# Graph network with a mixture of experts: column tiles for gathered edges, 19 dense buckets, earlier edge counts

## The chip, the cores and the metric

One core of one Trainium2 chip runs the whole model in one program. The metric is device time in microseconds of one execution. The engines are called PE (matrix products), DVE (vector), ACT (activations), POOL (GpSimd; it also writes the descriptors of indirect DMAs) and SP (it issues the plain DMAs).

## The reference, cut to what matters

There are 6250 nodes with 256 features and 100000 edges sorted by their destination. The edge list is the same in all edge stages.

```python
x = x + (segment_sum(w[:, None] * (ln(x) @ w_nbr)[src], dst) + ln(x) @ w_own + bias)   # first edge stage
x = x + moe(ln(x))                    # router, best 2 of 8 experts, 256 -> 1024 -> 256
h = ln(x)
for i in range(3):                    # three convolution passes
    t = h @ W[i]
    h = segment_sum(t[row] * norm[:, None], col, n) + b[i]   # edges and one loop per node
    h = relu(layernorm(h) * gamma[i] + beta[i])
x = x + h
x = x + slice_attention(ln(x))
```

The norm is the product of the inverse roots of both ends' degrees. All is float32.

## The kernel before

**Tiling.** Nodes lie in NT = 49 tiles ("buckets") of 128; edges, in order of destination, in ET = 782 tiles of 128. A gathered edge tile costs one indirect DMA by POOL (128 rows of 1 KB of `table`, by `step_src`), a one-hot of the destinations made by DVE (`lane` equal to `step_dst`), and one matmul on PE that multiplies the transposed one-hot with the rows. G = 4 edge tiles in a row add up in one bank; they can touch two buckets, so DVE adds the bank twice into `ACC` with two masks (`add_group`), at an offset that `bucket_offsets` loads into registers.

**Stages in order.** `prologue` turns the lists, computes the first table and counts whether the lists fit the fixed plan (`bad`, `apart`; here they do). `first_steps` runs the first edge stage over all 782 edge tiles (`steps_and_route`; ring of 32 row slots) with the router beside it; SP clears the count matrix `A` in pieces there (`clear`). `mixture` is `place` (slot numbers), `invert` (lists by slot) and `experts` (56 blocks of 256 slots; PE on two layers, POOL fetches tokens and puts results). `convolutions` begins with `combine` and then runs `layers_hybrid`; `slices` is the last part.

**Dense buckets.** The first F = 17 buckets of a pass are not gathered. `A` in DRAM holds for each of them the edge counts between every source tile and the bucket. POOL builds it by indirect DMAs that add 128 ones each (`edges`, in `experts`, 4 chains, 264 of them; the places come from `dense_places` on DVE in the first block). In a pass SP loads pieces of 7 matrices (`piece`, 8 buffers) and PE multiplies them with the scaled features kept in `X`: 17 x 49 = 833 matmuls a pass.

**The order in a pass.** `layers_hybrid` writes the order of each engine out by the steps s from TD = 264 to 781, one gathered tile each; there are GT = 518. `quota(s)` says how many dense matmuls are done by step s: 40 ahead, the rest evenly to DENSE_END = 738. `batches` gives each pair of buckets a step `at` after its last edge or its bank; from there DVE runs the node work in fixed distances (sums, statistics, root on ACT, scale, shift), PE the `turns` at `at + 14` and `products` at `at + 18`, SP the `store` of the next table at `at + 21`, and the `refill` of `X`. PE's queue is in program order. The row ring has RG = 24 slots, freed by four matmuls at a time; POOL starts the next pass when all of the next table has been stored. The last pair of buckets is worked on after the last step.

## Time and profile before

| | us |
|---|---|
| runs, median of 3 | 4598.39 (4594.6 to 4601.92) |
| profiled execution, its own time | 4596.34 |
| its span | 4594.6 |
| PE busy | 3891.9 (85%) |
| POOL busy | 2871.1 (62%) |
| DVE busy | 2100.5 (46%) |
| ACT busy | 866.6 (19%) |
| mean granted clock of PE | 0.91 |

The span runs from the first to the last instruction of the profiled execution. A busy share is an average over stages whose limits differ, so the views by stage and by time are read beside it. An indirect DMA is shown on POOL with the time in which POOL writes its descriptors; the transfer itself is not in it. A float32 matmul appears as two recorded matmuls, and their ends are modelled, so starts say more than durations.

### The profile page before, as it was taken

To read this page: it belongs to the slowest core of one execution; us is meant where nothing else is said; L and a number is where in the kernel's file an instruction comes from. 1 tells how busy PE (TensorE), PEld (TensorE's weight loads), DVE (VectorE), ACT (ScalarE), POOL (GpSimd) and SP (SyncE) were. 2 spreads that over 40 slices of the span, in tenths; PEclk is the share of its full clock that TensorE was granted. 3 is DMA by queue.
4 is the path that set the end of the run, shared out by engine and by line. 5 is a ranking of instruction groups with operands and counts; after the bars stand their busy time and mean duration, and the time that the engine had idled before them with its cause. 6 is when DMAs were issued, how large, how long until landed. Compare 5 with 4: busy or idle time off the path is not lost. (4 is left out here: it accounts for less than half of the span.)

```text
span 4594.6 us, 52816 instructions
## 1 busy us (share of the span) xinstructions
PE 3891.9 (85%) x16777; PEld 3209.9 (70%) x16777; DVE 2100.5 (46%) x6813; ACT 866.6 (19%) x2121; POOL 2871.1 (62%) x2846
## 2 busy tenths in 40 slices
PE   5656666666699999995899998999998999995988
PEld 4544444444488888884788887888886877774657
DVE  5444444454611111116345455454554555555974
ACT  1233333333122222223001011001011000000322
POOL 0377777777168778880677776777776777774000
PEclk8877677777799999997999999999998999997998
DMA  3355555555266666668766666666666666662001
GB/s 106 105 170 168 168 167 164 168 168 167 65 181 188 190 188 188 192 171 272 227 203 200 204 199 208 207 202 202 201 204 204 206 202 204 199 188 69 0 12 57
DMA packets 422939, 779.23 MB, mean 170 GB/s; under 512 B 106971, under 2 KB 264194, under 8 KB 422722
## 3 DMA queue, kind: packets, MB, share of 16 engines
q1 hardware_dynamic: 255078, 433.81, 29.0%
q0 software_dynamic: 160992, 336.12, 26.3%
q10 hardware_dynamic: 6652, 6.67, 0.5%
q8 instruction: 104, 1.70, 0.2%
q14 instruction: 113, 0.93, 0.1%
HBM read 655.55 MB, written 114.39 MB: 168 GB/s over the span
## 5 line engine op out<-in xcount | busy, mean ns | idle before, releaser
L2142 POOL DMA_INDIRECT rows_h<-table,step_src x1554 | 1487.7, 957 | 638.1 <-issue 562.0
L2182 PE MATMUL bank_g<-X,piece_h 128*128 128x256 f32 x4998 | 1314.3, 380 | 14.3 <-DMA piece_h<-edges_A 14.3
L2182 PEld LDWEIGHTS bank_g<-X,piece_h 128*128 128x128 f32 x4998 | 952.0, 190 | 144.8 <-issue 14.7
L2197 PE MATMUL bank_g<-rows_h,hot_h 128*128 128x256 f32 x3108 | 939.7, 390 | 77.6 <-DMA rows_h<-table,step_src 76.9
L887 POOL DMA_INDIRECT rows_r<-table,step_src x782 | 743.1, 950 | 359.3 <-issue 339.2
L912 PE MATMUL bank_r<-rows_r,hots_r 128*128 128x257 f32 x1564 | 578.7, 531 | 382.3 <-ACT rows_r L897 382.0
L2238 DVE TENSOR_SCALAR hot_h<-lane,step_dst 128x128 f32<-128x128 f32 x1554 | 458.6, 302 | 838.4 <-PE bank_g L2197 812.0
L912 PEld LDWEIGHTS bank_r<-rows_r,hots_r 128*128 128x128 f32 x1564 | 394.2, 266 | 546.2 <-ACT rows_r L897 456.0
L2197 PEld LDWEIGHTS bank_g<-rows_h,hot_h 128*128 128x128 f32 x3108 | 591.9, 194 | 193.9 <-DMA rows_h<-table,step_src 116.2
L923 DVE TENSOR_SCALAR hots_r<-lane,step_dst 128x128 f32<-128x128 f32 x782 | 233.9, 306 | 503.2 <-PE bank_r L912 488.9
L1704 POOL DMA_INDIRECT edges_A<-one_d,place_d x264 | 413.4, 1566 | 80.5 <-issue 80.5
L897 ACT ACTIVATE rows_r<-rows_r,step_w 128x256 f32<-128x256 f32 x782 | 339.7, 498 | 639.3 <-DMA rows_r<-table,step_src 639.2
L1663 PE MATMUL pH_e<-xe_e,w_e 128*128 128x256 f32 x1792 | 397.7, 380 | 2.5 <-DMA b_e<-in_L_ffn_b 2.5
L1678 PE MATMUL pY_e<-w_e,h_e 128*128 128x256 f32 x1792 | 396.0, 379 | 0.0
L956 DVE SCALAR_TENSOR_TENSOR ACC<-bank_g,mask,ACC 128x256 f32 x780 | 339.5, 477 | 102.7 <-issue 80.8
L1663 PEld LDWEIGHTS pH_e<-xe_e,w_e 128*128 128x128 f32 x1792 | 341.6, 191 | 49.6 <-issue 2.9
L1678 PEld LDWEIGHTS pY_e<-w_e,h_e 128*128 128x128 f32 x1792 | 336.1, 190 | 43.4
L1638 ACT ACTIVATE h_e<-pH_e,prm_e 128x256 f32<-128x256 f32 x448 | 187.8, 470 | 630.6 <-PE pH_e L1663 630.6
L1606 DVE TENSOR_SCALAR xe_e<-pT_e,prm_e 128x256 f32<-128x256 f32 x114 | 56.7, 539 | 372.6 <-PE pT_e L1670 362.8
L2219 ACT ACTIVATE sd_g<-mv_g,eps 128x2 f32<-128x2 f32 (+1 forms) x75 | 22.1, 295 | 1016.3 <-DVE mv_g L2266 1016.3
L1623 DVE TENSOR_TENSOR y_e<-pY_e,b_e 128x256 f32<-128x256 f32 x112 | 42.3, 419 | 322.4 <-PE pY_e L1678 322.4
L956 DVE SCALAR_TENSOR_TENSOR ACC<-bank_r,mask,ACC 128x257 f32 x392 | 170.7, 477 | 18.0 <-issue 15.3
(318 smaller groups left out, 3039.7 us busy)
## 6 DMA issues: line engine op xcount, KB each, us to landing
piece_h<-edges_A SPq DMA_DIRECT2D x357, 448.0 KB, 3.6
w_e<-in_L_ffn_W SPq DMA_DIRECT2D x112, 1024.0 KB, 8.1
edges_A<-zero_r SPq DMA_DIRECT2D x119, 448.0 KB, 4.9
rows_h<-table,step_src POOLq DMA_INDIRECT x1554, 3.3
got_c<-y SPq DMA_DIRECT2D x14, 896.0 KB, 9.6
rows_r<-table,step_src POOLq DMA_INDIRECT x782, 2.8
table<-ACC SPq DMA_DIRECT2D x48, 256.0 KB
X<-table SPq DMA_DIRECT2D x12, 896.0 KB, 12.1
```

The lines of the kernel that those rows point to most:

```text
L887: nc.gpsimd.indirect_dma_start(out=r["rows"][:, x, 0:D], out_offset=None, in_=r["table"][:, :], in_offset=bass.IndirectOffsetOnAxis(ap=c[" ...
L897: act.activation(r["rows"][:, x, 0:D], r["rows"][:, x, 0:D], ACT.Copy, scale=c["step_w"][:, k:k + 1]).then_inc(r["s_scaled"], 1)
L912: pe.matmul(psum[k // G % OH][:, 0:AW], r["hots"][:, k % HOTS, :], r["rows"][:, k % R, 0:AW], start=(k % G == 0), stop=(k % G == G - 1 or ...
L923: v.tensor_scalar(r["hots"][:, k % HOTS, :], c["lane"][:, :], c["step_dst"][:, k:k + 1], None, ALU.is_equal).then_inc(r["s_hot"], 1)
L956: v.scalar_tensor_tensor(out=a, in0=bank[:, 0:width], scalar=c["mask"][:, k, g:g + 1], in1=a, op0=ALU.mult, op1=ALU.add).then_inc(c["ring" ...
L1663: mm = pe.matmul(pH[j][:, n * BR:(n + 1) * BR], w1[:, q, k, o:o + P], xe[:, q, k, :], start=(k == 0), stop=(k == KD - 1))
L1678: mm = pe.matmul(pY[m][:, 0:D], h[:, j, m * P:(m + 1) * P], w2[:, q, j, :], start=(j == 0), stop=(j == HJ - 1))
L1704: nc.gpsimd.indirect_dma_start(out=dram["A"][:, :], out_offset=bass.IndirectOffsetOnAxis(ap=d["place"][:, col:col + 1], axis=0), in_=d["on ...
L2142: nc.gpsimd.indirect_dma_start(out=d["rows"][:, x, :], out_offset=None, in_=tables[l - 1][:, :], in_offset=bass.IndirectOffsetOnAxis(ap=c[ ...
L2182: mm = pe.matmul(pD[o % 2][:, 0:D], d["piece"][:, n % AB, x % PC, :], c["X"][:, ORDER[x // PC] * PC + x % PC, :], start=(x == 0), stop=(x ...
L2197: pe.matmul(pS[i // G % OH][:, 0:D], d["hot"][:, i % HOTS, :], d["rows"][:, x, :], start=(i % G == 0), stop=(i % G == G - 1 or i == GT - 1 ...
L2238: v.tensor_scalar(d["hot"][:, i % HOTS, :], c["lane"][:, :], c["step_dst"][:, TD + i:TD + i + 1], None, ALU.is_equal).then_inc(r["s_hot"], 1)
```

## The change

1. **Column tiles.** In the three passes a one-hot has 32 columns (destination modulo 32, `step_low`). Groups have GB = 8 edge tiles; two in a row (GP = 2) go to one of four column positions of the array (`tile_position`), so four sums of 32 lanes stand in one bank (`lanes`). DVE copies the bank to `mid` and makes a one-hot `spread` from `target`, the bucket lane of each of the 128 partial rows (`kept`); PE multiplies them (`spread`), which puts the rows in their lanes, and DVE adds the product twice with masks (`added`). There are 61 groups a pass. The prologue makes `step_low` and `target` and checks the list for this form.
2. **Buckets.** F = 19, TD = 296, GT = 486 gathered tiles, 931 dense matmuls a pass, ending at step 754. Node work moves: turns at `at + 8`, products at `at + 10`, store at `at + 14`. The first five refills are issued one by one as the last bucket's matmuls pass, and no longer together after it.
3. **Edge counts.** 296 scatters. Ten are issued in `place`, 23 in `invert`, 263 in `experts`. `dense_places` runs in the first edge stage; SP loads its lists there; 133 pieces are cleared over the first 23 of 25 batches.
4. **Combining** is pipelined by a group: sums of group g + 1 come before the normalisation of group g; a refill of `X` by ACT copies takes the place of a DMA.

```diff
-F = 17
+F = 19
-GG = -(-GT // G)
+GB, GP = 8, 2
+GG = -(-GT // GB)
+LOW = P // 4
-DENSE_END = 738
+DENSE_END = 754
+EARLY = (10, 33)
...
+                elif t == 7:
+                    then(v.tensor_scalar(base_i[:, 0, :], base[:, 0, :], -1.0, part[:, 0:1], ALU.mult, ALU.add))
+                    then(v.tensor_scalar(base_i[:, 1, :], base_i[:, 0, :], LOW - 1, None, ALU.bitwise_and))
+                    then(v.tensor_copy(base[:, 1, :], base_i[:, 1, :]))
+                    then(v.tensor_tensor(base_i[:, 0, :], base[:, 0, :], base[:, 1, :], ALU.add))
+                    then(v.tensor_scalar(base_i[:, 1, :], base_i[:, 0, :], P - 1, None, ALU.bitwise_and))
+                    v.tensor_copy(c["target"][:, :], base_i[:, 1, :])
...
         @block.gpsimd
         def _(g):
+            numbers(nc, d)
             run_pool(nc, c, r, g)
...
+                if i == LAG and u == 12:
+                    dense_places(v, c, d)
...
+            g.wait_ge(c["s_clear"], 16 * PIECES)
+            for n in range(EARLY[0]):
+                edges(nc, g, dram, d, n)
...
+            for n in range(*EARLY):
+                edges(nc, g, dram, d, n)
...
+            def kept(g):
+
+                act.wait_ge(c["s_x2"], 16 * (g + 1))
+                act.wait_ge(q["h"], g * TG + TG)
+                for t in range(g * TG, (g + 1) * TG):
+                    i = act.activation(c["X"][:, t, :], c["ACC"][:, t, 0:D], ACT.Copy)
+                i.then_inc(c["s_hd"], 16)
...
+            added(0)
+            for g in range(NG):
+                if g + 1 < NG:
+                    added(g + 1)
+                normalised(g)
...
-                        if l < LAYERS and s == at + 21:
+                        if l < LAYERS and s == at + 14:
                             store(l, k)
...
-                    if i % Q == 0 and i >= RG:
-                        g.wait_ge(r["s_mm"], n - RG + Q)
+                    if i % GB == 0 and i >= RG:
+                        g.wait_ge(r["s_mm"], n - RG + GB)
...
+            def lanes(l, h):
+
+                n, tiles = ET + (l - 1) * GT, tiles_of(h)
+                m = (l - 1) * GG + h
+                for x in sorted({i % RG // Q for i in tiles}):
+                    last = max(i for i in tiles if i % RG // Q == x)
+                    pe.wait_ge(r["s_row"][x], 16 * (BEFORE[x] + (l - 1) * EACH[x] + landed(last, GT, RG, x)))
+                pe.wait_ge(r["s_hot"], n + tiles[-1] + 1)
+                if m >= 2:
+                    pe.wait_ge(d["s_mid"], m - 1)
+                for i in (*tiles[0::GP], *tiles[1::GP]):
+                    k = i % GB // GP * LOW
+                    pe.matmul(pA[m % 2][k:k + LOW, 0:D], d["hot"][:, i % (2 * GB), :], d["rows"][:, i % RG, :],
+                              start=(i % GP == 0), stop=(i % GP == GP - 1), tile_position=(0, k)).then_inc(r["s_mm"], 1)
+
+            def spread(l, h):
+
+                m, k = (l - 1) * GG + h, rows_of(h)
+                pe.wait_ge(d["s_mid"], m + 1)
+                if m >= 2:
+                    pe.wait_ge(r["s_add"], 2 * (EG + m - 1))
+                pe.matmul(pR[m % 2][:, 0:D], d["spread"][0:k, m % 2, :], d["mid"][0:k, m % 2, :],
+                          start=True, stop=True).then_inc(d["s_spread"], 1)
...
+                    s = TD + i
+                    if i % GB == 0:
+                        lanes(l, i // GB)
+                        if i >= GB:
+                            spread(l, i // GB - 1)
                     dense(l, AHEAD_MM if i == 0 else quota(s - 1), quota(s))
                     if l < LAYERS:
                         for k, (_, _, at) in enumerate(GROUPS):
-                            if s == at + 14:
+                            if s == at + 8:
                                 turns(l, k)
-                            if s == at + 18:
+                            if s == at + 10:
                                 products(l, k)
+                spread(l, GG - 1)
...
+            def kept(l, h):
+
+                m, k = (l - 1) * GG + h, rows_of(h)
+                v.wait_ge(r["s_mm"], ET + (l - 1) * GT + tiles_of(h)[-1] + 1)
+                v.tensor_scalar(d["spread"][:, m % 2, :], c["lane"][:, :], c["target"][:, h:h + 1], None, ALU.is_equal)
+                v.tensor_copy(d["mid"][0:k, m % 2, :], pA[m % 2][0:k, 0:D]).then_inc(d["s_mid"], 1)
...
+                    s, h = TD + i, i // GB
+                    if i % GB == 0 and h >= 1:
+                        kept(l, h - 1)
+                        if h >= 2:
+                            added(l, h - 2)
+                    if i + GB < GT:
+                        hot(i + GB)
```

## Rows read from the trace of the kernel before

**Rows 1.** The page: busy tenths in 40 slices, two engines.
```profile
PE   5656666666699999995899998999998999995988
...
POOL 0377777777168778880677776777776777774000
```

**Rows 2.** Windows by stage: us, busy us (instructions) by engine, PEclk, DMA share, GB/s.
```profile
1242.30:2081.00 838.70, 805.62 (x3812) 702.37 (x3812) 114.78 (x297) 189.04 (x449) 637.10 (x491) 0.99 0.67 185
2081.00:2199.50 118.50, 70.43 (x296) 51.60 (x296) 77.56 (x252) 49.23 (x112) 0.00 (x0) 0.80 0.88 288
2199.50:2872.50 673.00, 650.17 (x3010) 568.23 (x3011) 332.64 (x1073) 62.96 (x172) 495.88 (x518) 0.98 0.68 207
```

**Rows 3.** The page, groups: busy us, mean ns, idle before and its releaser.
```profile
L2142 POOL DMA_INDIRECT rows_h<-table,step_src x1554 | 1487.7, 957 | 638.1 <-issue 562.0
...
L1704 POOL DMA_INDIRECT edges_A<-one_d,place_d x264 | 413.4, 1566 | 80.5 <-issue 80.5
```

**Rows 4.** Timeline, POOL: start us, us, line, operation, idle before; gathers at pass ends.
```profile
2199.56 0.99 POOL L2142 DMA_INDIRECT rows_h<-table,step_src  x1 [126.95 <-issue]
...
2852.03 0.95 POOL L2142 DMA_INDIRECT rows_h<-table,step_src  x1 [0.30 <-issue]
2872.57 0.94 POOL L2142 DMA_INDIRECT rows_h<-table,step_src  x1 [19.59 <-DMA table<-ACC]
```

**Rows 5.** Timeline, PE: back to back in pass 1, and after a wait.
```profile
2610.71 0.59 PE L2197 MATMUL bank_g<-rows_h,hot_h 128*128 128x256 f32 x2
2611.14 0.59 PE L2182 MATMUL bank_g<-X,piece_h 128*128 128x256 f32 x2
...
4201.61 1.13 PE L2197 MATMUL bank_g<-rows_h,hot_h 128*128 128x256 f32 x4 [0.16 <-DMA rows_h<-table,step_src]
```

**Rows 6.** Groups by line of PE alone, 2223 to 2816 us (dense part of pass 1).
```profile
L2182 PE MATMUL bank_g<-X,piece_h 128*128 128x256 f32 x1589 | 420.5, 379 | 0.0
L2197 PE MATMUL bank_g<-rows_h,hot_h 128*128 128x256 f32 x949 | 282.4, 379 | 0.0
L2165 PE MATMUL bank_g<-w_g,xt_h 128*128 128x256 f32 x168 | 39.7, 379 | 0.0
L2155 PE MATMUL bank_g<-ident,xin_h 128*128 128x128 f32 x84 | 12.6, 273 | 0.0
```

**Rows 7.** Timeline, PE: first gathered matmuls of passes 1 and 2.
```profile
2223.41 0.59 PE L2197 MATMUL bank_g<-rows_h,hot_h 128*128 128x256 f32 x2
...
2886.78 0.59 PE L2197 MATMUL bank_g<-rows_h,hot_h 128*128 128x256 f32 x2
```

**Rows 8.** Timeline, all engines: the end of pass 1.
```profile
2855.07 1.06 PE L2155 MATMUL bank_g<-ident,xin_h 128*128 128x128 f32 x4
...
2856.16 0.66 ACT L2227 ACTIVATE xt_h<-bank_g 128x256 f32<-128x256 f32 x2 [10.34 <-PE bank_g L2155]
...
2857.41 1.89 PE L2165 MATMUL bank_g<-w_g,xt_h 128*128 128x256 f32 x8
...
2858.64 0.88 DVE L956 SCALAR_TENSOR_TENSOR ACC<-bank_g,mask,ACC 128x256 f32 x2 [0.24 <-DVE ACC L956]
```

**Rows 9.** Timeline, DVE: list work in the prologue.
```profile
54.31 0.54 DVE L389 CAST lane_i_a<-dcol 128x782 int32<-128x782 f32 x1
...
65.25 0.97 DVE L409 TENSOR_TENSOR falls<-now_i,next_i 128x782 f32<-128x782 int32 x1 [2.22 <-DMA deg_i<-in_dst]
```

**Rows 10.** Timeline, POOL and DVE: constants and ends of placing and inversion, an iota.
```profile
1176.83 0.29 POOL L1383 TENSOR_SCALAR_AFFINE_SELECT before<-ones 128x128 f32<-128x128 f32 x1
...
1194.75 0.19 DVE L1464 TENSOR_SCALAR moe_expert<-ebf 128x57 int32<-128x57 f32 x1
...
1241.78 0.22 DVE L1529 TENSOR_SCALAR moe_put<-dest_i 128x112 int32<-128x112 f32 x1
...
1242.27 0.36 POOL L1708 IOTA aside_d<- 128x264 f32 x1 [46.56 <-POOLq L1472]
```

**Rows 11.** Timeline, DVE: after ACT's root in the last group of the combining.
```profile
2178.79 0.20 DVE L1821 RECIPROCAL rs_g<-sd_g 128x7 f32<-128x7 f32 x1 [2.41 <-ACT sd_g L1858]
```

More of the change, by code:

```diff
@@ L68 @@
 GT = ET - TD
-GG = -(-GT // G)
+GB, GP = 8, 2
+GG = -(-GT // GB)
+LOW = P // 4
+EP = -(-ET // GP)
 RG = 24
@@ L97, in batches @@
 def batches():
-    out = [(t, 2, 16 * (t + 2) + SLACK) for t in range(F, NT - 2, 2)]
+    out = [(t, 2, 16 * (t + 2) + 2 * GB) for t in range(F, NT - 2, 2)]
     taken = [s for _, _, s in out]
@@ L103, in batches @@
         s = bucket_done(t + n - 1) + 3
-        while min(abs(s - x) for x in taken) < 12:
+        while min(abs(s - x) for x in taken) < 10:
             s += 1
@@ L154, in build @@
             prologue(nc, ins, dram, c, sb, pb, sem)
+            d = dict(place=sb("place_d", [P, TD], I32, g), one=sb("one_d", [P, TD], F32, g), s_ed=sem("d_ed"), s_ix=sem("d_ix"),
+                     s_acc=[sem(f"d_acc{k}") for k in range(CHAINS)])
             apart = nc.values_load(c["apart"][0:1, 0:1], min_val=0, max_val=1,
@@ L327, in _ @@
             pe.wait_ge(s_kept, 1)
-            pe.matmul(pH[:, 0:EG], firsts[:, :], dcol[:, 0:EG * G:G], start=True, stop=True).then_inc(s_head, 1)
+            pe.matmul(pH[:, 0:EP], firsts[:, :], dcol[:, 0:EP * GP:GP], start=True, stop=True).then_inc(s_head, 1)
             turn(0)
@@ L1020, in token_rows, with numbers, route_sync @@
     sp.dma_start(rows[:, bass.ds(t, n), :], c["X"][:, bass.ds(t, n), :]).then_inc(q["rows"], 16)
-def route_sync(sp, ins, dram, moe, b, q):
+def numbers(nc, d):
+    nc.gpsimd.iota(d["aside"][:, :], [[1, TD]], base=0, channel_multiplier=TD,
+                   allow_small_or_imprecise_dtypes=True).then_inc(d["s_ed"], 16)
+def route_sync(sp, ins, dram, moe, b, d, q):
+    for name in ("src", "dst"):
+        sp.dma_start(d[name][:, :], ins[name][0:ED].rearrange("(p n) -> p n", p=P)).then_inc(d["s_ed"], 16)
     sp.dma_start(b["wr"][:, :, :], ins["L0_ffn_Wr"].rearrange("(k p) e -> p k e", p=P)).then_inc(q["w"], 16)
@@ L1263, in _ @@
             sp.wait_ge(c["s_clear"], 16 * PIECES)
+        @block.gpsimd
+        def _(g):
+            numbers(nc, d)
         @block.vector
@@ L1341, in _, with place @@
                     mm.then_inc(q["L"], 1)
-def place(nc, c, moe, sb, pb, sem):
+def place(nc, dram, c, moe, d, sb, pb, sem):
     with ExitStack() as ctx:
@@ L1544, in _, with edges, experts @@
             body(NG - 1)
-def experts(nc, ins, dram, c, moe, sb, pb, sem):
+def edges(nc, g, dram, d, n):
+    k, x = n // CHAINS, n % CHAINS
+    col = x * (TD // CHAINS) + k
+    if k == 0:
+        g.wait_ge(d["s_ix"], PLACED)
+    else:
+        g.wait_ge(d["s_acc"][x], 16 * k)
+    nc.gpsimd.indirect_dma_start(
+        out=dram["A"][:, :], out_offset=bass.IndirectOffsetOnAxis(ap=d["place"][:, col:col + 1], axis=0),
+        in_=d["one"][:, col:col + 1], in_offset=None, compute_op=ALU.add).then_inc(d["s_acc"][x], 16)
+def experts(nc, ins, dram, c, moe, d, sb, pb, sem):
     with ExitStack() as ctx:
@@ L1697, in results @@
                         in_=y[:, b % 2, m, :], in_offset=None).then_inc(s_st[b % 2], 16)
-            def edges(n):
-                k, x = n // CHAINS, n % CHAINS
-                col = x * (TD // CHAINS) + k
-                wait(g, s_acc[x], 16 * k)
-                nc.gpsimd.indirect_dma_start(
-                    out=dram["A"][:, :], out_offset=bass.IndirectOffsetOnAxis(ap=d["place"][:, col:col + 1], axis=0),
-                    in_=d["one"][:, col:col + 1], in_offset=None, compute_op=ALU.add).then_inc(s_acc[x], 16)
-            nc.gpsimd.iota(d["aside"][:, :], [[1, TD]], base=0, channel_multiplier=TD,
-                           allow_small_or_imprecise_dtypes=True).then_inc(s_ed, 16)
             for b in range(4):
@@ L1806, in convolutions @@
                          xt=sb("xt_h", [P, 2, D], F32, own))
-                d.update(rows=sb("rows_h", [P, RG, D], F32, own), hot=sb("hot_h", [P, HOTS, P], F32, own),
+                d.update(rows=sb("rows_h", [P, RG, D], F32, own), hot=sb("hot_h", [P, 2 * GB, LOW], F32, own), mid=sb("mid_h", [P, 2, D], F32, own),
+                         spread=sb("spread_h", [P, 2, P], F32, own),
                          piece=sb("piece_h", [P, AB, PC, P], F32, own), bank=bank)
@@ L2070, in dinv, with tiles_of, rows_of @@
         return c["dinv"][:, t:t + 1]
+    def tiles_of(h):
+        return range(h * GB, min(h * GB + GB, GT))
+    def rows_of(h):
+        return -(-len(tiles_of(h)) // GP) * LOW
     def used(l, s):
@@ L2258, in stats @@
                 v.wait_ge(q["z"], (l - 1) * NT + FIRST[k] + n)
+                if l == LAYERS and k > 0:
+                    v.wait_ge(q["zz"], 3 * FIRST[k])
                 for u in range(n):
@@ L2350, in _ @@
                         nodes(l, k, s - at)
+                for h in range((GT + 1) // GB, GG):
+                    kept(l, h)
+                for h in range((GT + 1) // GB - 1, GG):
+                    added(l, h)
                 v.wait_ge(r["s_add"], 2 * (EG + l * GG))
```

208 lines of the change are left out of this document (115 added, 93 removed).

## The prediction

> **What bounds the kernel now.** I read the slices of the page first. PE is at 8 to 9 tenths from the expert stage on, and POOL stands at 7 wherever it issues indirect DMAs [rows 1]. Both look busy and neither looks full, so the slices don't settle it. The windows by stage give the sizes: the experts 839 us, the combining 118.5 us, then three convolution passes alike, of which the first has 673 us at a granted clock of 0.98 [rows 2]. The change lies mostly in the three passes, so I looked there for what ends last.
>
> POOL issues one gather per edge tile. One takes 957 ns [rows 3], and the next starts after 0.30 us: 1.25 us from start to start, without a stall. Pass 1 runs from its first gather at 2199.56 to its last at 2852.03, that is 652.5 us for 517 intervals, 1.262 us each [rows 4]; the passes 2 and 3 have the same 518 gathers at the same mean, and I count three times 652.5, 1957.5 us. The 562 us of "issue" ahead of the gathers [rows 3] look like idle time, but most of it is this 0.30 us, paid 1,500 times. POOL therefore sets the passes. Between two passes it stands still, 20.54 us from start to start, waiting for the table to be stored [rows 4].
>
> PE is hardly less loaded. One 128x128 by 128x256 float32 matmul is two recorded matmuls, and the next one starts 0.43 us later (2610.71 to 2611.14; its pair takes 0.59 us, which is 2 x 0.216 and a tail of 0.16) [rows 5]. From 2223 to 2816, the dense part of pass 1, no PE group has any idle time before it [rows 6]. That stretch holds 793 dense and 474 gathered matmuls and node work for 42 tiles. Node work is 8 halves a pair (1.73 us) and 4 half transposes (about 0.44 us), so 1.08 us a tile and 45 us in all; (593 - 45) / 1267 = 0.4325 us a matmul, the same number again. So PE has no reserve either: POOL leads, PE is just full. That is the reason why a cheaper gathered matmul counts here and why more dense work alone would not pay.
>
> **The passes.** Two buckets more go from gathered to dense. TD goes from 264 to 296, so gathers fall from 518 to 486 per pass. If POOL still leads, a pass is 485 x 1.262 = 612.1 us, and three are 1836.3 instead of 1957.5 us: 121.2 us less.
>
> Now PE. In eight steps POOL needs 10.1 us. PE has to do: dense, 891 matmuls over 458 steps, 15.56 x 0.4325 = 6.73 us (now 13.38, 5.79 us); nodes, about 45 tiles x 1.08 over 57 groups, 0.85 us; one new spread matmul, 0.43 us. These make 8.02 us. To it comes the group of eight gathered tiles, each now a matmul with 32 stationary columns, placed in four column positions. The trace has no matmul in a column tile, so its cost is bounded. From above: nothing overlaps, eight times 0.4325 is 3.46 us, since the moving side still streams 256 columns. From below: four abreast, 0.87 us. I take two abreast, 8 x 0.216 and one more half, 1.95 us, because each float32 product is two halves on one column tile, the second half follows the first, and only the neighbour's first half can run beside it. It is an assumption; the nearest row is the back-to-back pair of halves [rows 5].
>
> Going from full to column use and back may empty the array. After a wait four halves took 1.13 us [rows 5] instead of 4 x 0.216 = 0.86 (tail included), so a restart is 0.27 us. A group has none, one or two of them; I take one. Then eight tiles cost 2.2 us and PE needs 10.24 us per eight steps.
>
> The rows show a tail and a restart price, but nothing that changes the shape of the array. The Trainium skill, "TensorEngine Tiling (Array Packing)", section "Tiling Modes", says that changing the tiling mode drains the engine; that speaks against the change and asks for both restarts, a rival below. The Trainium skill, "TensorE: Matmul & The Clock Gate", section "Part 3: Packing small matmuls", gives 2.38x for three column tiles; worked out from that page, an estimate, eight tiles would be 1.45 us, and every pass would stay with POOL. No row here shows either.
>
> A pass lasts, if PE leads, from the first gather: PE's lag at its first gathered matmul (2223.41 - 2199.56 = 24 us in pass 1, 2886.78 - 2872.57 = 14 us later [rows 4, 7]), plus 57 groups, plus about 8 us for the last six gathers, which wait for slots of the ring of 24. Pass 1: 24 + 57 x 10.24 + 8 = 616 us, against 612 of POOL. Pass 2: 606 us, so POOL's 612.1. Pass 3 has no transposes and products, 9.39 us per group: POOL. Sum 1840 us, a gain of 117.5 us. What covers the 98 dense matmuls more in a pass (42 us) is only the cheap group; if that cover goes, they are on the path at once.
>
> DVE: one-hots of 32 columns in place of 128 are no dearer than 0.30 us, and per eight steps it now adds one group pair instead of two; two new operations (about 0.7 us) replace them. It has time. New waits: DVE waits for a whole group of matmuls before it copies (the hot tiles of the next group are issued before that, so PE is not starved), PE's spread waits for that copy one group later, SP's refills wait for bank use in five steps. Queued behind SP's waits are the pieces, with eight buffers, 28 steps of dense work. I cost these waits at nothing while PE's group takes 10 us. DMA in the passes is at 0.68 [rows 2]; the bytes rise a few per cent in less time, to about 0.75, hidden likewise.
>
> **The ends of the passes.** Now the turns of the last but one pair run while rows are awaited, and the last add starts at 2858.64 [rows 8]. After the change PE's order is: last group, spread of the group before, turns and products of the pair due at 768, and only then the last spread. From the end of the last group that is 0.43 + 1.1 (four half transposes) + 0.66 and 0.2 (ACT copy) + 1.89 (products) [rows 8] and 0.6 for the spread, 4.9 us; before, the add came about 1 us after the last matmul. The chain from there to the next gather is as before. 4.2 us more, twice: +8.4. After pass 3 there are no products: +1.
>
> **The rest.** Prologue: DVE runs without a break there and gets about a dozen operations more: two of 486 columns (below the 0.54 us of one of 782 [rows 9]), wider head copies, a chain of six at about 0.2 us. About 4.5 us, of which a DMA wait takes 2.2 us [rows 9]: +2.5 (0 to +5). First pass: one iota ahead of the gathers, +0.4 [rows 10]; the place arithmetic moved there from the experts is 5 us of DVE under a POOL that never waits, and 14 more clears go over SP at a DMA load of about half: nothing. Slots: ten scatters at 1.57 + 0.30 us [rows 3] make 18.7 us behind POOL's constants, which end at 1177.12; so 1195.8, and DVE is done at 1194.94 [rows 10]: +1.3. Inversion: 23 scatters, 43 us from 1195.7, end at 1239, while DVE ends at 1242.0 [rows 10]: nothing, at most +4 if full DVE work slows POOL. Experts: 263 scatters instead of 264, 4.87 a block at 1.87 us and four other DMAs of about 1.28 us, 14.2 us of POOL in 15.0 us a block (839 / 56 [rows 2]), as now; iota gone ahead of the first fetch: -0.7.
>
> Combining: DVE idles 2.4 us per group for ACT's root [rows 11], seven times. The pipelining takes that out, but ACT gets 49 copies (2.8 us a group) in place of a DMA, and has about 7 x 1.2 us of its own a group. So ACT takes over the pace at 12 to 12.5 us, where about 13.5 us a group stand now (118.5 us [rows 2] less some 24 us ahead of and behind the seven). An extra 9 us of filling at the start eats most of it. -3, from -12 to +5.
>
> Sum: -117.5 + 8.4 + 1 + 2.5 + 0.4 + 1.3 - 0.7 - 3 = -107.6. The profiled execution took 4596.34 us (span 4594.6), 2 us below the median of 4598.39. So 4488.7; I say 4489.
>
> **The rivals.** *Serial column tiles*: the change doesn't do what it says, matmuls in different column positions run one after another. Eight tiles cost 3.46 us and one restart, 3.73. PE per group 11.75 us: pass 1 702, pass 2 692, pass 3 (10.9 us) 644, in sum 2038, +80.5; with the other terms 4686 us (4640 without restarts, 4731 with two). It decides from 3.2 us per eight tiles, 0.40 us a tile: above it the kernel is slower. For it speaks that 0.4325 is what the streaming of the moving operand costs in this trace at any weight; against it, that weight loads already run beside matmuls. Chance 0.19.
> *Half the overlap*: eight tiles at 2.9 us, PE leads in passes 1 and 2 (654 and 645 us), pass 3 612: gain 46.5, time 4560. Chance 0.14.
> *Both restarts*, the mechanism of the drain, full to column and back, each 0.27 us: PE 10.5 us per group, passes 631, 620 and 612, time 4512. Chance 0.15.
> *POOL leads throughout* (up to four abreast, no restart seen) is within the forecast: 4485. Forecast with it 0.52.
>
> **How the numbers follow.** Forecast 4489, from 4467 (all passes with POOL, prologue free, combining -12) to 4510. Adding the second and third rival brings the held chance to 0.8; the range is 4467 to 4562. About 0.2% (9 us) is what a measurement tells from no change. Slower by more than that: the serial case less its edge, 0.18. Within: 0.04, the stretch near 0.40 us a tile. Faster: 0.78.
>
> **What would show it.** POOL's gathers still 1.26 us apart to the end of each pass, 612 us from first to last: right. Gathers that wait for PE, in passes 1 and 2 but not in 3: PE leads, and starts of PE's column matmuls a half apart (0.216) or less, 0.11, or a full 0.43 tell which rival. The gap between passes at 24.7 us. No scatter ending after DVE in the inversion. I would be wrong if gathers slow down by themselves at the higher DMA load, or if PE waits for DVE's copies.

## The result and the profile after the change

The changed kernel takes 4487.34 us (median of four runs, 4485.14 to 4489.91), the kernel before 4596.5 us beside it (4593.27 to 4601.92): a ratio of 0.9762 with a 95% interval of 0.9745 to 0.9778. The profiled execution has a span of 4487.6 us against 4594.6 before, 107.0 us less. The forecast was 4489.

The page, the busy tenths of two engines and the granted clock in 40 slices; [rows 1] has the same slices of before:

```profile
PE   5656555656589999996799998899997888885988
POOL 0377777777657778774277777577776777773000
PEclk9887778777799999998999999899998999997988
```

They look like those of before, and that is the first thing to read: the same engines work at the same shares, over a shorter time. Groups by line (busy us, mean ns | idle before, and what ended it); the gathers answer to [rows 3], the rest to [rows 6]:

```profile
L2233 POOL DMA_INDIRECT rows_h<-table,step_src x1458 | 1393.7, 956 | 613.9 <-issue 565.4 <-DMA table<-ACC 48.2 <-PE bank_g L2290 0.3
L2273 PE MATMUL bank_g<-X,piece_h 128*128 128x256 f32 x5586 | 1262.3, 382 | 11.7 <-DMA piece_h<-edges_A 11.7
L2290 PE MATMUL bank_g<-rows_h,hot_h 128*32 128x256 f32 x2916 | 213.5, 410 | 195.4 <-issue 187.9 <-DMA rows_h<-table,step_src 7.1
L2299 PE MATMUL bank_g<-mid_h,spread_h 128*128 128x256 f32 (+1 forms) x366 | 141.4, 472 | 0.0
```

GpSimd (POOL) issues 1458 gathers instead of 1554 at the same 956 ns. In all three passes it waits 0.3 us for TensorE (PE) and 48.2 us for the table between passes, and for nothing else: it leads ("issue" is its own 0.30 us between two gathers, and the time ahead of the first). TensorE has 195.4 us of idle time ahead of the gathered products (L2290). The profile puts most of it down to "issue"; it is the wait for rows: at the end of pass 1 the last gather starts at 2813.00, the page has 3.6 us from a gather's issue to its landing, and the last group starts at 2816.55. From 2223 to 2816 us of pass 1 these waits are 43.7 us, where before had none in the same stretch [rows 6].

Windows of pass 1 with the gap behind it, and of 300 us in its middle (us, busy us and instructions of PE, PEld, DVE, ACT, POOL, then granted clock, DMA share, GB/s); [rows 2] has before's:

```profile
2201.80:2838.73 636.93, 575.65 (x3266) 457.74 (x3267) 252.90 (x1035) 62.97 (x172) 464.37 (x487) 0.96 0.72 222
2351.80:2651.80 300.00, 280.54 (x1628) 225.07 (x1627) 123.54 (x504) 32.02 (x88) 227.48 (x239) 0.99 0.72 218
```

TensorE is busy 280.5 of 300 us: GpSimd leads, and TensorE has 6 to 7% in reserve. The pass and its gap are 636.9 us, where 673.0 us stood.

Two groups of eight gathered tiles in that stretch, timeline of PE (start, duration, line):

```profile
2558.22 1.07 PE L2290 MATMUL bank_g<-rows_h,hot_h 128*32 128x256 f32 x16
2559.22 0.70 PE L2299 MATMUL bank_g<-mid_h,spread_h 128*128 128x256 f32 x2
2559.76 6.64 PE L2273 MATMUL bank_g<-X,piece_h 128*128 128x256 f32 x30
2566.32 1.07 PE L2290 MATMUL bank_g<-rows_h,hot_h 128*32 128x256 f32 x16
2567.33 0.70 PE L2299 MATMUL bank_g<-mid_h,spread_h 128*128 128x256 f32 x2
2567.86 4.48 PE L2273 MATMUL bank_g<-X,piece_h 128*128 128x256 f32 x20
```

The 16 halves of eight products take 1.07 us with their tail. Their starts come in fours: 0, 0.007, 0.013 and 0.020 us, then 0.240 to 0.260, 0.456 to 0.476, 0.672 to 0.692. Four positions of the array work side by side. The last dense half starts at 2566.02 and is due to be done with its 0.216 us at 2566.23, so the eight tiles hold TensorE for 1.09 us until the spreading product starts; 0.10 us more pass before the dense products go on (2567.33 + 2 x 0.216 = 2567.76, against 2567.86). So 1.20 us in all, changes between whole array and columns among it.

Where the 107 us are, by stage, from the starts in the two traces:

| stage | before | after | measured | forecast |
|---|---|---|---|---|
| to the first gather | 178.9 | 176.5 | -2.4 | +2.9 |
| first gathers (782) | 980.1 | 980.4 | +0.3 | 0 |
| last of them to the first expert product (slots, inversion) | 96.5 | 102.2 | +5.7 | +0.6 |
| experts, first to last product | 813.5 | 816.5 | +3.0 | 0 |
| combining, up to the first gather of pass 1 | 130.7 | 126.2 | -4.5 | -3 |
| three passes, first to last gather | 1957.5 | 1834.1 | -123.4 | -117.5 |
| two gaps between passes | 40.4 | 50.1 | +9.7 | +8.4 |
| behind the last gather | 397.1 | 401.6 | +4.5 | +1 |

### The profile page after: what moved, and what is told of

It is laid out like the page before. It is cut to its first block and busy times, and to the rows that moved or that the text cites. A ratio compares the mean times of both kernels' runs of the same rounds, so it can differ in the third digit from the quotient of the medians.

```text
span 4487.6 us, 54073 instructions
## 1 busy us (share of the span) xinstructions
PE 3621.3 (81%) x17539; PEld 2865.8 (64%) x17539; DVE 1868.7 (42%) x6689; ACT 873.3 (19%) x2164; POOL 2828.6 (63%) x2783
## 5 line engine op out<-in xcount | busy, mean ns | idle before, releaser
L2233 POOL DMA_INDIRECT rows_h<-table,step_src x1458 | 1393.7, 956 | 613.9 <-issue 565.4
L2273 PE MATMUL bank_g<-X,piece_h 128*128 128x256 f32 x5586 | 1262.3, 382 | 11.7 <-DMA piece_h<-edges_A 11.7
L2273 PEld LDWEIGHTS bank_g<-X,piece_h 128*128 128x128 f32 x5586 | 1070.3, 192 | 161.0 <-issue 13.3
L939 PE MATMUL bank_r<-rows_r,hots_r 128*128 128x257 f32 x1564 | 553.3, 511 | 410.0 <-ACT rows_r L924 409.6
L1604 POOL DMA_INDIRECT edges_A<-one_d,place_d x296 | 464.1, 1568 | 90.3 <-issue 90.3
L2290 PE MATMUL bank_g<-rows_h,hot_h 128*32 128x256 f32 x2916 | 213.5, 410 | 195.4 <-issue 187.9
L2350 DVE TENSOR_SCALAR hot_h<-lane,step_low 128x32 f32<-128x32 f32 x1458 | 274.2, 254 | 17.2 <-issue 17.2
L2290 PEld LDWEIGHTS bank_g<-rows_h,hot_h 128*32 128x32 f32 x2916 | 89.7, 113 | 292.5 <-issue 263.1
L2357 DVE TENSOR_SCALAR spread_h<-lane,target 128x128 f32<-128x128 f32 x183 | 56.1, 307 | 466.3 <-PE bank_g L2290 466.2
L983 DVE SCALAR_TENSOR_TENSOR ACC<-bank_g,mask,ACC 128x256 f32 x366 | 159.9, 479 | 76.6 <-issue 58.1
```

Source lines behind the costliest of these rows:

```text
L939: pe.matmul(psum[k // G % OH][:, 0:AW], r["hots"][:, k % HOTS, :], r["rows"][:, k % R, 0:AW], start=(k % G == 0), stop=(k % G == G - 1 or ...
L1604: nc.gpsimd.indirect_dma_start(out=dram["A"][:, :], out_offset=bass.IndirectOffsetOnAxis(ap=d["place"][:, col:col + 1], axis=0), in_=d["on ...
L2233: nc.gpsimd.indirect_dma_start(out=d["rows"][:, x, :], out_offset=None, in_=tables[l - 1][:, :], in_offset=bass.IndirectOffsetOnAxis(ap=c[ ...
L2273: mm = pe.matmul(pD[o % 2][:, 0:D], d["piece"][:, n % AB, x % PC, :], c["X"][:, ORDER[x // PC] * PC + x % PC, :], start=(x == 0), stop=(x ...
L2290: pe.matmul(pA[m % 2][k:k + LOW, 0:D], d["hot"][:, i % (2 * GB), :], d["rows"][:, i % RG, :], start=(i % GP == 0), stop=(i % GP == GP - 1) ...
L2350: v.tensor_scalar(d["hot"][:, i % (2 * GB), :], c["lane"][:, 0:LOW], c["step_low"][:, i:i + 1], None, ALU.is_equal).then_inc(r["s_hot"], 1)
```

## The experiments

Twelve kernels ran. Four of them (e5 to e8) had a chip on which the kernel before took 4597.3 us, as usual. The other eight had two chips on which it took 5050 us (e1 to e4) and 5079 us (e9 to e12); I call them disturbed. Their first stage, which no variant touches, lasted 1112 to 1121 us instead of 980. Their microseconds are therefore not compared with 4487, only their ratios to before on the same chip, and what their traces show of single engines. The changed kernel itself did not run on these two chips, so no ratio measured there can be set against the change's 0.9762. What is known of the disturbance stands at the end. Of the numbers that follow, those marked as ratios carry their 95% interval.

### Are four column tiles really four abreast?

e1 puts all gathered tiles in one column position:

```diff
-                for i in (*tiles[0::GP], *tiles[1::GP]):
-                    k = i % GB // GP * LOW
+                for i in tiles:
+                    k = 0
```

with `rows_of` returning `LOW`, so that the spreading product takes 32 rows alone.

> The changed kernel, but all gathered tiles in the first of the four column positions (no two can run side by side), written to the first 32 lanes of the bank; the spreading product takes those 32 lanes alone, so the aggregates of three quarters of the gathered tiles are wrong. If the eight lane products are cheap because four positions work at once (16 halves in 1.07 us, starts of four 7 ns apart, the next four 0.215 us later), the 16 halves now stand one behind the other: 16 x 0.215 = 3.4 us, 2.4 us more for each of 61 groups, 145 us more of TensorE per pass; TensorE then leads all three passes: 4740 us, 4700 to 4780. If the products are cheap for their 32 columns of weights and not for their positions, it stays at 4488.

Measured: 5004 us (two runs), ratio 0.991 (0.9877 to 0.9943). PE's timeline, and the window of pass 1 with its gap:

```profile
2614.59 3.64 PE L2290 MATMUL bank_g<-rows_h,hot_h 128*32 128x256 f32 x16
2618.16 0.69 PE L2299 MATMUL bank_g<-mid_h,spread_h 32*128 32x256 f32 x2
2341.24:3107.36 766.12, 738.73 (x3266) 523.51 (x3267) 251.87 (x1035) 63.09 (x172) 468.75 (x487) 0.98 0.60 185
```

The same 16 halves take 3.64 us, one behind the other with 0.216 us between starts. The 32 columns of weights save nothing; the four positions do. From the dense half before them to the one behind the spreading product a group costs 2.66 us more than with four positions. TensorE's recorded busy time for a pass and its gap is 738.7 us, but such times come out longer on the disturbed chips (more on that under e4), so I work the serial rival out from spacings, an estimate: 931 dense products at 0.4325 us, 61 groups at 3.86 us, 61 spreading products at 0.43 us and 53 us of node work (49 tiles at 1.08) are 717 us in passes 1 and 2, and 664 us in pass 3 without node work. The changed kernel needs 636.9, 634.0 and 613.3 us with all its waits. So TensorE would lead everywhere, and the kernel would take about 4700 us or more: the serial rival of the prediction was real as a mechanism. e10 is the same kernel once more:

> The kernel of one column position again (aggregates of three quarters of the gathered tiles wrong), since the chip of its first run held every kernel up at gathers that landed late: there a group of 16 halves took 3.64 us against 1.07 to 1.09 in four positions. By that price, 2.55 us more for each of 61 groups, 156 us more of TensorE in a pass, and it leads all three: passes with their gaps of 637 us become some 730, the third 680: 4740 us (4700 to 4780). If GpSimd's gathers still led, 4488.

It had a disturbed chip too: 5041 us, ratio 0.9931 (0.9902 to 0.9961), with 740.9 us of TensorE in pass 1. The total of this rival on an undisturbed chip was not measured.

e2 keeps the positions and issues the eight products in the order of the tiles, so that neighbours have the same position: `for i in tiles:` alone.

> The changed kernel with the eight lane products of a group issued in the order of the tiles, 0 1 2 ... 7, so that each two neighbours have the same column position. If TensorE starts products in the order of issue and one waits for the last of its position, the eight take five steps of 0.43 us instead of two: 2.2 us instead of 1.07, 1.2 us per group, 70 to 75 us of TensorE per pass; passes 1 and 2, with about 575 us busy in 637, become some 20 to 30 us longer each, the third hardly: 4540 us (4515 to 4560). If the order does not matter (the engine takes whichever position is free): 4488.

Measured: 5026 us, ratio 0.996 (0.9941 to 0.9979). PE's timeline:

```profile
2613.75 1.09 PE L2290 MATMUL bank_g<-rows_h,hot_h 128*32 128x256 f32 x16
```

1.09 us, not 2.2. The starts are again four together (0, 0.014, 0.027, 0.040, then 0.240 to 0.280). The first four halves in order of issue all have the same position here, and e1 shows that halves of one position start 0.216 us apart. So my picture, that a product waits at the head of one queue for its own position, is wrong: products of other positions behind it start beside it. The order of the tiles is not what gives the overlap. The time of the whole kernel settles nothing: 0.996 lies above what either case was to give (4540 and 4488 us are ratios of 0.988 and 0.976), and TensorE stood still for 139 of the 766 us of pass 1 with its gap. Whether the order costs something elsewhere stays open.

### Which part of the change pays?

e3 has everything but the two buckets:

```diff
-F = 19
+F = 17
...
-DENSE_END = 754
+DENSE_END = 738
```

> The changed kernel with 17 dense buckets as before (dense products ending at step 738), so: column tiles, early scatters and the new combining alone. If GpSimd's gathers lead every pass at 1.251 us a tile, 32 more tiles cost 40 us a pass, 120 us in three, and the column tiles alone give nothing: 4607 us (4595 to 4612), no faster than the kernel before. If the relief of TensorE alone had shortened a pass, it would be at 4560 or less.

Measured: 5077 us, ratio 1.0059 (1.0042 to 1.0076), on the disturbed chip; once more as e11:

> 17 dense buckets with the column tiles and all the rest of the change, again, on a chip where gathers land in time: 518 tiles at 1.251 us a pass instead of 486, 40 us a pass: 4600 us (4590 to 4610), the time of the kernel before within 0.3%. If column tiles shortened a pass by themselves: 4560 or less.

5111 us, ratio 1.0062 (1.0046 to 1.0079), on the other disturbed chip. Twice 0.6% slower than before: on these chips the column tiles with the early scatters and the new combining give nothing by themselves. I had expected within 0.3%; where the other 0.3% go I can't say. For a chip where gathers land in time the trace of before says the same: they already went out 1.262 us apart there [rows 4], and a cheaper product can't shorten that.

e4 has the two buckets and everything else, but the gathered path of before, one product of 128 columns per tile, with the node work at its old distances (turns at `at + 14`, products at `at + 18`, store at `at + 21`):

```diff
...
-                pe.matmul(pA[m % 2][k:k + LOW, 0:D], d["hot"][:, i % (2 * GB), :], ...
+                pe.matmul(pS[i // G % OH][:, 0:D], d["hot"][:, i % HOTS, :], d["rows"][:, x, :],
...
```

> The changed kernel with the gathered path of before (one product of 128 columns a tile, no lanes and no spreading, groups of four) and 19 dense buckets. If TensorE has no room for two more buckets without column tiles: 11.0 us of it for eight steps against 10.0 of GpSimd in passes 1 and 2, 664 and 654 us instead of 611 and 610, the third pass at GpSimd's 612, the two gaps between passes 4 to 5 us shorter each: 4575 us (4560 to 4595). If GpSimd leads here too: 4480, and the column tiles were not needed.

> 19 dense buckets with the gathered path of before, again, on a chip where gathers land in time: if TensorE leads passes 1 and 2 without the column tiles (11.0 us for eight steps against 10.0), 664 and 654 us instead of 611 and 610, gaps 4 to 5 us shorter: 4575 us (4555 to 4595). If GpSimd leads: 4480.

Measured: 4932 and 4956 us, ratios 0.9765 (0.9749 to 0.9781) and 0.9764 (0.9747 to 0.978). So on the disturbed chips two buckets more pay without column tiles, and nothing shows that column tiles help there: e2, the changed kernel but for its order of issue, stood at 0.996 on the chip on which e4 stood at 0.9765. GpSimd's gathers of a pass are 1.45 to 1.56 us apart on average in all of e1 to e4 and e9 to e12, not by their number alone: in e4's passes GpSimd waits 223.6 us for TensorE to free row slots and 104.5 us for a releaser that the profile calls "remote". Window of e4's pass 1 with its gap:

```profile
2345.30:3090.11 744.81, 697.34 (x3140) 596.83 (x3141) 302.90 (x1027) 62.77 (x172) 468.40 (x486) 0.97 0.62 190
```

TensorE is recorded busy for 697.3 us of it, for 689.2 in the next pass and 641.5 in the third. That can't be carried over to a chip where gathers land in time: e2, whose products are those of the changed kernel, has 627.3, 620.1 and 597.6 us on the same chip, where the changed kernel has 575.7, 576.1 and 518.8. From the 0.4325 us of the trace of before, an estimate: 931 + 486 products are 612.9 us and the node work of 49 tiles 52.9 us. So TensorE has at least 665.8 us of work in passes 1 and 2 and 612.9 in pass 3, against the 636.9, 634.0 and 613.3 us that the changed kernel needs with all its waits. TensorE would lead passes 1 and 2, and e4 would be at least 61 us above the changed kernel: 4548 us or more. With the 23 us in which TensorE stands still in pass 1 and its gap before ([rows 2]: 673.0 less 650.17) in both, it is 4594, the time of the kernel before; my 4575 lies between. That the column tiles are needed for more than half of the gain is therefore worked out, not run.

### What do the early scatters cost and give?

e5: `EARLY = (0, 0)`, all 296 scatters beside the experts.

> The changed kernel with all 296 edge-count scatters in the experts' stage, none ahead of it. GpSimd is nearly full there (616 us busy and 140 of issue in 774, 18 us waiting for VectorE): 33 more at 1.57 + 0.31 us are 62 us, 18 of them hidden: experts 44 us longer, and the slots' and the inversion's 5 to 6 us come back: 4526 us (4510 to 4545). If TensorE's experts hide them: 4481, and the early scatters cost time without need.

Measured: 4533.0 us (4527.1 to 4534.5), ratio 0.9861 (0.9846 to 0.9876), 45.7 us more than the change; the experts take 56.1 us more, the two stages ahead of them 6.2 less and the combining 4.4 less. GpSimd's timeline in the changed kernel (the last scatter beside the slots, the first constant of the inversion, the last scatter beside the inversion, the experts' first fetch), then in e5:

```profile
1192.91 1.56 POOL L1604 DMA_INDIRECT edges_A<-one_d,place_d  x1 [0.30 <-issue]
1196.66 0.24 POOL L1537 IOTA token<- 128x98 f32 x1 [2.19 <-ACTq L1519]
...
1239.18 1.59 POOL L1604 DMA_INDIRECT edges_A<-one_d,place_d  x1 [0.30 <-issue]
1247.09 1.01 POOL L1739 DMA_INDIRECT tok_e<-tokens,moe_inv  x1 [6.33 <-POOLq L1519]
```

```profile
1173.42 0.17 POOL L1420 IOTA node<- 128x49 f32 x1 [16.46 <-SPq L1391]
1192.35 0.24 POOL L1537 IOTA token<- 128x98 f32 x1 [18.10 <-ACTq L1519]
1240.05 0.98 POOL L1739 DMA_INDIRECT tok_e<-tokens,moe_inv  x1 [47.22 <-POOLq L1519]
```

Slots: 18.9 us from the constants to the inversion without scatters, 22.0 with ten (1174.63 to 1196.66). Inversion: 47.7 us without, 50.4 with 23. That is the +5.7 us of the table. Beside the slots the last scatter ends at 1194.47, 0.4 us after VectorE's last operation, and the inversion starts 2.2 us later; without scatters it starts 0.3 us after VectorE's last. In the inversion the scatters are over 6.3 us before the experts start, so GpSimd isn't late; what is late is VectorE. Its two operations that make the lists (L1559 and L1560, 98 each) take 309 and 382 ns on average beside the scatters, 277 and 329 in e5. Most are as quick as there, but in 20 of the 23 scatters one L1560 that starts some 0.54 us into it takes 0.59 us instead of 0.33, and one L1559 at 0.78 us takes 0.40 instead of 0.28. Waits of PE in the experts' stage, 1300 to 2060 us, in the changed kernel and in e5 (total us, times, longest):

```profile
PE pT_e L1721 <- DMA tok_e<-tokens,moe_inv: 10.9, 15, 1.7
```

```profile
PE pT_e L1721 <- DMA tok_e<-tokens,moe_inv: 50.3, 35, 3.6
```

With all scatters there TensorE waits 50.3 us for its tokens, and the stage takes 872.6 us instead of 816.5: 1.70 us for each of 33 scatters, nearly the full 1.87 of one. I had expected 44 us for the stage, with 18 hidden; 56 came. It works on the other side too: with 231 scatters instead of 263 (e3, e11) the stage took 802.0 and 801.9 us on the disturbed chips, where every kernel with 263 took 815 to 819. So GpSimd is partly on the path of the experts in the changed kernel as well, and 32 scatters fewer would be worth up to 14.5 us there.

### The combining, and the last spreading product

e6 puts the combining stage of before into the changed kernel.

> The changed kernel with the combining stage of before (one moments buffer, each group added and normalised in turn, the residual copied by DMA). The traces have the stage at 133.2 us after and 137.6 before: 4492 us (4490 to 4494), 0.1% longer. If that difference came from the stages around it: 4487.

Measured: 4494.5 us (4493.1 to 4498.7), ratio 0.9783 (0.977 to 0.9797), 7.2 us more. In its trace the stage takes 130.7 us, as before, against 126.2: the 4.5 us of the table come from the combining's own code. The other 2.7 us have no place in the trace and are within what runs differ by.

e7 issues the last spreading product one step after its lanes:

```diff
+                    if i == (GT - 1) // GB * GB + 1:
+                        spread(l, GG - 1)
-                spread(l, GG - 1)
```

> The changed kernel with the last spreading product of a pass issued one step after its lanes, ahead of the node products of the pair due at step 768, instead of behind them. In the trace that product starts 6.1 us after the one before it, behind two node operations, one of 3.75 us: if it is on the path that ends a pass, each of the two gaps between passes is 4 to 5 us shorter, the step after the third pass 0 to 2: 4478 us (4475 to 4483). If the node products' pair is late instead and takes its place: 4487.

Measured: 4483.7 us (4480.7 to 4486.5), ratio 0.9759 (0.9746 to 0.9773), 3.7 us less by the medians, which the runs alone don't tell from nothing (the intervals of the two ratios overlap nearly whole). The trace does: the gaps are 22.4 and 21.5 us instead of 25.7 and 24.4, 6.2 us less together. The end of pass 1 in the changed kernel, then in e7:

```profile
2816.55 1.93 PE L2290 MATMUL bank_g<-rows_h,hot_h 128*32 128x256 f32 x12 [5.18 <-issue]
2818.41 1.22 PE L2299 MATMUL bank_g<-mid_h,spread_h 128*128 128x256 f32 x2
2819.42 1.06 PE L2246 MATMUL bank_g<-ident,xin_h 128*128 128x128 f32 x4
...
2820.95 3.75 PE L2256 MATMUL bank_g<-w_g,xt_h 128*128 128x256 f32 x8 [0.47 <-ACT xt_h L2339]
2824.53 0.61 PE L2299 MATMUL bank_g<-mid_h,spread_h 96*128 96x256 f32 x2
2825.28 0.88 DVE L983 SCALAR_TENSOR_TENSOR ACC<-bank_g,mask,ACC 128x256 f32 x2 [4.63 <-PE bank_g L2299]
...
2838.73 0.94 POOL L2233 DMA_INDIRECT rows_h<-table,step_src  x1 [24.79 <-DMA table<-ACC]
```

```profile
2813.00 1.93 PE L2290 MATMUL bank_g<-rows_h,hot_h 128*32 128x256 f32 x12 [4.79 <-issue]
2816.73 1.06 PE L2299 MATMUL bank_g<-mid_h,spread_h 96*128 96x256 f32 x2
2817.58 2.39 PE L2256 MATMUL bank_g<-w_g,xt_h 128*128 128x256 f32 x8
2817.93 0.88 DVE L983 SCALAR_TENSOR_TENSOR ACC<-bank_g,mask,ACC 128x256 f32 x2 [0.83 <-PE bank_g L2299]
2831.91 0.95 POOL L2233 DMA_INDIRECT rows_h<-table,step_src  x1 [21.50 <-DMA table<-ACC]
```

From the last lanes to the last add it was 8.7 us and is 4.9. The order of two instructions is worth 3 us a gap; of the 3.8 us in the first gap 0.5 are given back behind it.

### How far does it go?

e8 has 21 dense buckets, and the 32 further scatters in a new GpSimd block of the combining stage, where it was idle:

```diff
-F = 19
+F = 21
...
+COMBINED = 32
...
-            late = TD - EARLY[1]
+            late = TD - EARLY[1] - COMBINED
...
+        @block.gpsimd
+        def _(g):
+            for n in range(TD - COMBINED, TD):
+                edges(nc, g, dram, e, n)
...
```

The wait for the end of all scatters moves there too.

> The changed kernel with 21 dense buckets; the 32 further scatters stand in the combining stage, where GpSimd is idle. If GpSimd's gathers lead the passes at 1.251 us with TensorE close behind: 32 tiles fewer, 40 us a pass, 4368 us. If TensorE takes the lead in passes 1 and 2 (575 us busy, 37 more of dense products, 8 less of lanes, 605 against a pass and gap of 597 at GpSimd's pace): about 17 us gained in each of these and 40 in the third, 0 to 10 lost in combining: 4415 us (4405 to 4435). This one is the forecast.

Measured: 4396.9 us (4394.5 to 4400.6), ratio 0.9569 (0.9554 to 0.9584), 90.4 us below the changed kernel and below my range. Windows inside passes 1 and 2, and GpSimd's waits in the passes:

```profile
2370.00:2570.00 200.00, 200.00 (x1145) 162.50 (x1143) 81.30 (x328) 23.00 (x63) 144.95 (x152) 1.00 0.74 225
2985.00:3185.00 200.00, 200.00 (x1142) 162.73 (x1145) 77.29 (x316) 21.91 (x60) 151.68 (x159) 1.00 0.76 231
POOL rows_h L2239 <- issue: 407.1, 1336, 0.5
POOL rows_h L2239 <- DMA table<-ACC: 51.2, 2, 25.8
POOL rows_h L2239 <- PE bank_g L2296: 31.6, 23, 2.3
```

TensorE is busy 200 us of 200, and GpSimd now waits for it, 31.6 us in 23 places. The passes are 589.0, 579.2 and 575.2 us, where the gathers alone would take 453 x 1.251 = 567. So TensorE has the lead in passes 1 and 2 at 21 buckets, as expected, but it costs less of the gain: 22 and 30 us came off them, not 17 each. And the combining hides its 32 scatters whole (126.5 us against 126.2). This is the test of what leads: 32 gathers fewer per pass bring 22, 30 and 38 us, of 40.

e9 is e8 with the order of e7 and `AHEAD_MM = 54` instead of 40.

> 21 dense buckets with the 32 further scatters in the combining stage, the last spreading product of a pass ahead of the pair's node products, and 54 instead of 40 dense products ahead of a pass's first gathered tile. With 21 buckets TensorE was busy without a gap in the middle of passes 1 and 2 (200 us of 200), so what is moved into the gap before the pass comes off it: 14 x 0.38 = 5 us in each of the first two passes, and 3 us in each gap for the spreading product: 4382 us (4372 to 4392). If the products ahead only push the first lanes back, 4390 or more.

It had a disturbed chip: 4846 us, ratio 0.9538 (0.9522 to 0.9554), the lowest ratio of all. Its interval touches that of e8, and the chips differ, so whether it is faster than e8 is open. The best kernel that is shown is e8, 2.0% below the change.

## Why the prediction was right

**The passes.** "POOL leads, PE is just full" holds, and the first step of the sum with it: 485 intervals at 1.262 us were to give 612.1 us; measured 611.2, 609.6 and 613.3. The gathers are as far apart as before and 32 fewer, so the gain comes from their number and not from the cheaper products. e8 shows that it goes on while TensorE has room, and e3 and e11 fit, on chips where gathers are further apart. What the cheap products are for, to keep TensorE from leading, is shown by its 280.5 us of 300; how much would be lost without them is the estimate under e4. Two signs that would have spoken against me didn't come: the spreading products have no idle time ahead of them (L2299, 0.0 us), so TensorE doesn't wait for VectorE's copies, and the gathers don't slow down at a DMA share of 0.72 instead of 0.68.

**The eight tiles.** This term was mis-sized. "I take two abreast" put them at 1.95 us and a restart of 0.27, 2.2 us in all; they take 1.20 us. From above (3.46 us) and below (0.87 us) the bounds were right, e1 measured the upper one as 3.64 with its tail, and the value was the lower. The reason I gave for two abreast, the second half behind the first in one queue, is what e2 contradicts. Because of it I had TensorE leading pass 1 by 4 us (616), which it does not. TensorE's eight steps are 6.73 + 0.85 + 0.43 + 1.20 = 9.2 us instead of 10.24; the window above says 280.5 / 300 of 10.0, 9.4. The error cost 4 us of the forecast and put 0.29 of chance on two rivals (half overlap, both restarts) that were nowhere near.

The restart: between dense products and lanes 0.09 us are lost, within the lanes and up to the spreading product 0.14, and 0.10 on the way out. My 0.27 was a misreading too: the 1.13 us of four halves after a wait [rows 5] hold the recorded tail of 0.16, the 0.86 beside them don't. Four halves with their tail are 1.02 us, so those rows give 0.11 for a restart; with it POOL would have led pass 1 in my own sum, even at two abreast, and both restarts would hardly have been a rival. The Trainium skill, "TensorEngine Tiling (Array Packing)", section "Tiling Modes", says that a change of mode drains the engine; the trace doesn't show a drain as such, and each of the two changes costs here about what a restart after a wait costs without one, 0.1 us.

**The ends of the passes.** Forecast +8.4, measured +9.7: the order named there (last group, spread of the group before, turns, products, last spread) is the order of the rows above, but the eight halves of the products took 3.75 us and not 1.89, since TensorE had waited for rows and stood at its lower clock (granted 0.50 from 2816.5 to 2824.5; the 12 lane halves took 1.93 us, where 16 take 1.07 at full clock). My +4.2 a gap was also 0.3 more than the terms beside it give (4.9 less 1). With the other order in e7 the gaps are 43.9 us in sum, against 50.1, and 40.4 before: two thirds of the added time is the order, the rest is open.

**The slots, inversion and experts.** The sum had +1.3, 0 and -0.7; measured +5.7 for these and +3.0 in the experts. "At most +4 if full DVE work slows POOL" looked the wrong way round: the scatters slow VectorE. And where I had the slots end with the last scatter, 2.2 us more pass before the inversion starts. For the experts "14.2 us of POOL in 15.0 us a block" was right as an average and hid that single blocks are over it; e5 and e3 measure the slope, 1.70 and 0.45 us a scatter on either side of 263. Why the stage is 3.0 us longer with one scatter fewer stays open (TensorE waits 10.9 us for tokens there, 9.0 before; other kernels with 263 scatters on the usual chip took 814.5 to 815.9).

**The rest.** Prologue: +2.9 expected, -2.4 measured; the added VectorE work is there (97.4 us busy in the first 180 us against 91.3), but TensorE had the higher clock level for more of this stretch (granted 0.96 against 0.87). I know of no cause in the change, and in e1 to e12 the first gather comes at 175.4 to 179.4 us, so this is within what executions differ by. Combining: -3 forecast, -4.5 measured, e6 confirms it. Behind the last gather +1 expected, +4.5 measured: the last add comes 1.6 us later, and folding the weights finds TensorE longer at its lower clock (16 half products in 3.78 us instead of 2.83; granted 0.61 against 0.71 in the some 53 us behind the last gather).

The single misses (+5.1 slots and inversion, +3.0 experts, +3.5 behind the last gather, +1.3 gaps, +0.3 first gathers; -5.9 passes, -5.3 prologue, -1.5 combining) cancel to 0.5 us. That the forecast came within 2 us is luck; the mechanism and the size of the passes are not.

## What to carry to other kernels

A cheaper operation on the engine that is second brings nothing by itself; what it brings is room, and the gain comes from the work that is moved into that room from the engine that leads (32 gathers a pass in the change, another 32 in e8; e3 and e11, with none moved, gained nothing). Measure the leading engine's reserve again after each step: here it lasted for two buckets with 7% to spare and for four with none. And look at what the last step of a stage waits behind in its own queue: an order of two instructions cost 3 us in each gap, and helpers that run beside a stage (scatters) are not free for the engine that they don't use.

## What the runs showed of the hardware that I had not expected

- Float32 products of 128 rows by 32 columns in four column positions: 16 halves of 256 columns each in 1.07 us, four starts 7 ns apart (13 ns where neighbours share a position, 1.09 us), against 3.64 us in one position. The order of issue changes 0.02 us of a group.
- Indirect scatters beside VectorE: in nearly every scatter one operation of 0.33 us takes 0.59 us, and the next of 0.28 us takes 0.40. With 23 scatters the inversion was 2.7 us longer.
- Chips differ: on two of them the kernel before took 10% longer (5050 and 5079 us against 4597). GpSimd's gathers pause there. In the first stage of e2, equal in all kernels, these are its waits from 200 to 1170 us; the changed kernel has 20.7 us for TensorE there and nothing of the other kind:

```profile
POOL rows_r L914 <- issue: 188.3, 616, 0.9
POOL rows_r L914 <- remote: 102.2, 35, 7.0
POOL rows_r L914 <- PE bank_r L939: 33.2, 30, 3.8
```

  In the eight traces 41 to 49 gathers of that stage wait over 1 us, 3.1 to 3.5 on average, mostly 16 or 20 gathers apart, 130 to 140 us in sum beyond the usual 0.30; the stage is 131 to 141 us longer. Other things keep their durations: scatters their 1.57 us in the kernels with 17 or 19 buckets, and the experts' stage with 263 scatters 815 to 819 us. In e2's pass 1 other engines pause at such moments too:

```profile
2624.72 0.60 PE L2246 MATMUL bank_g<-ident,xin_h 128*128 128x128 f32 x4
2631.30 0.29 DVE L2357 TENSOR_SCALAR spread_h<-lane,target 128x128 f32<-128x128 f32 x1 [6.73 <-remote]
2631.46 0.66 ACT L2339 ACTIVATE xt_h<-bank_g 128x256 f32<-128x256 f32 x2 [8.96 <-remote]
```

  ScalarE starts to copy 6.1 us after the transposes that it waits for have ended (2625.32), and VectorE resumes at the same moment, long after the lanes it waits for (2623.39). It looks as if signals between engines arrived late, all together; the profile has "remote" for the releaser, though one core alone runs the program, and the cause stays open.
